# State scan of a fused kernel: B and C rows loaded apart, block steps moved, and du*B of nine states made by ScalarE and TensorE

## The reference, cut to what matters

```python
def step(h, inp):
    d_t, B_t, C_t, u_t = inp
    dA = jnp.exp(d_t[..., None] * A)
    h = dA * h + (d_t * u_t)[..., None] * B_t[:, None, :]
    y = jnp.einsum('ben,bn->be', h, C_t)
    return (h, y)
```

## Time and profile before

| | us |
|---|---|
| median of 3 runs | 665.01 (663.41 to 665.39) |
| profiled execution, whole | 662.23 |
| its span, first to last instruction | 660.4 |
| state scan in it, from the first product to the end of the last scan | 229.27 to 472.1 |

### The profile page before, as it was taken

How to read it: one execution, slowest core, us unless ns; L and a number is a source line. 1 busy time by engine, 2 the same in 40 slices (tenths; PEclk the granted TensorE clock), 3 DMA queues, 4 the chain that set the end, 5 groups by cost and what they waited for, 6 DMA issues and landing times.

```text
span 660.4 us, 9558 instructions
## 1 busy us (share of the span) xinstructions
PE 529.6 (80%) x3244; PEld 415.0 (63%) x3244; DVE 453.6 (69%) x987; ACT 334.9 (51%) x622; POOL 374.9 (57%) x306
## 2 busy tenths in 40 slices
PE   8988888997959495559546966898787889898994
PEld 5666558996837353447345735543356789898974
DVE  3444682653613799979897999999868554545585
ACT  3444551442413679644984596788150344444444
POOL 1011106455455178997898599789641666566640
PEclk9989998997988887759965995899898999999997
DMA  4234002742121455544225434534100111111213
GB/s 128 76 137 161 30 1 58 254 156 60 49 53 51 126 192 175 171 165 161 106 103 189 140 129 131 176 133 154 48 18 4 41 41 45 41 40 43 73 62 94
DMA packets 33679, 66.29 MB, mean 100 GB/s; under 512 B 6449, under 2 KB 20342, under 8 KB 33120
## 3 DMA queue, kind: packets, MB, share of 16 engines
q1 hardware_dynamic: 27136, 44.31, 20.6%
q0 software_dynamic: 4768, 9.32, 5.6%
q10 hardware_dynamic: 1728, 12.06, 5.1%
HBM read 57.60 MB, written 8.52 MB: 100 GB/s over the span
## 4 chain that ended last, share of the span: by engine, by line
PE 39%; DVE 17%; POOL 15%; issue 13%; ACT 7%; another core or an unknown queue 6%; DMA 2%; POOLq 0%; DVEq 0%; ACTq 0%
POOL w L2119 6%; PE ps L762 5%; PE ps L734 5%; PE ps L770 5%; PE ps L746 4%; PE ps L738 4%; POOL wide L2119 4%; DVE wide L1978 3%; DVE ps L1971 2%; PE ps L828 2%; DVE w L1978 2%; DVE work L1650 1%; DMA w<-bc_rows 1%; POOL work L2081 1%
## 5 line engine op out<-in xcount | busy, mean ns | idle before, releaser
L2207 POOL DMA_INDIRECT rows<-xn_rows,source x78 | 77.0, 987 | 81.2 <-DVE place L1659 24.8
L1978 DVE TENSOR_TENSOR_SCAN wide<-work,ps 128x512 f32<-128x512 f32 x86 | 99.8, 1203 | 0.4 <-ACT work L1356 0.4
L1971 DVE TENSOR_TENSOR ps<-ps,w 128x512 f32<-128x512 f32 x128 | 81.6, 684 | 6.2 <-DMA w<-bc_rows 6.0
L2119 POOL TENSOR_TENSOR wide<-wide,w 128x1024 f32<-128x1024 f32 x22 | 52.0, 2362 | 28.0 <-DVE wide L1978 27.8
L1356 ACT ACTIVATE work<-work,a_neg 128x512 f32<-128x512 f32 x86 | 56.6, 710 | 14.2 <-DVE wide L1978 6.5
L1709 DVE TENSOR_TENSOR wide<-wide,ps 128x512 f32<-128x512 f32 x39 | 26.8, 687 | 51.3 <-PE ps L738 29.1
L926 PE MATMUL ps<-ident,w 128*128 128x128 f32 x192 | 36.7, 354 | 26.4 <-POOL w L2119 26.4
L1699 DVE COPY xT<-ps 128x128 f32<-128x128 f32 x78 | 22.1, 286 | 50.8 <-remote 23.9
L762 PE MATMUL ps<-xT,wide 128*128 128x128 f32 x312 | 44.9, 290 | 10.1 <-DVE xT L1699 8.3
L926 PEld LDWEIGHTS ps<-ident,w 128*128 128x128 f32 x192 | 30.2, 185 | 35.2 <-POOL w L2119 32.3
L926 PE MATMUL ps<-ident,wide 128*128 128x128 f32 x192 | 32.5, 325 | 24.4 <-POOL wide L2119 24.3
(11 more groups left out here) (347 smaller groups left out, 1261.7 us busy)
## 6 DMA issues: line engine op xcount, KB each, us to landing
w<-bc_rows SPq DMA_DIRECT2D x64, 512.0 KB, 3.8
w<-in_w ACTq DMA_DIRECT2D x2, 2304.0 KB, 9.2
wg<-in_wg ACTq DMA_DIRECT2D x1, 2304.0 KB
wu<-in_wu ACTq DMA_DIRECT2D x1, 2304.0 KB
wd<-in_wd ACTq DMA_DIRECT2D x4, 576.0 KB
w<-y_choice SPq DMA_DIRECT2D x8, 256.0 KB, 2.8
y_slots<-yout SPq DMA_DIRECT2D x20, 64.0 KB
rows<-xn_rows,source POOLq DMA_INDIRECT x78
```

The source lines that it names most:

```text
L1971: V.tensor_tensor(dbu[:, h, :], du[:, h, :], bc_all[j % 4][:, 0:S], ALU.mult).then_inc(dbu_set, 1)
L1978: V.tensor_tensor_scan(st[n % 3][:, h, :], dA[n % 3][:, h, :], dbu[:, h, :], 0.0, ALU.mult, ALU.add).then_inc(st_set if h else st_half, 1)
L2119: G.tensor_tensor(hc[j % 4][:, 0:own, :], st[n % 3][:, 0:own, :], bc_all[j % 4][:, S:2 * S].unsqueeze(1).to_broadcast([P, own, S]), ALU.mu ...
L2207: G.indirect_dma_start(out=xin[i % RING][:, :], out_offset=None, in_=xn_rows, in_offset=bass.IndirectOffsetOnAxis(ap=source[:, i:i + 1], a ...
```

## The change

B and C rows are loaded by two DMAs of 256 KB each. B's waits for VectorE's product (`dbu_set`), C's for GpSimd's (`hc_set`), and C's of a state waits in SyncE's program for B's of the same state to have landed.

In nine states the product du*B is made otherwise (`TERM_AT`). Once per block TensorE transposes du (time onto partitions) and B, and ScalarE copies both to SBUF (`turn_du`, `turn_b`, `keep_turned`). For such a state, ScalarE multiplies the four turned tiles by a column of B as its scale (`weigh_term`), and TensorE transposes the result back into `dbu`, four tiles for each half (`turn_term`), each half after the scan of the state before that reads it. VectorE then issues no product in that state.

Steps move: `gate_sum` j = 1 to 2, `take_back` 3 to 4, `take_rows` 4 to 5, `row_stats` 5 to 6, `activate` 5 to 6, `take_low` and `project_low` 6 to 7, `soft_parts` and `project_dt` 7 to 8, `apply_norm` 10 to 11, `project_z` from 10 and 11 to 9 and 10, the first part of `step_size` 8 to 9, `scale_fetched(3)` 5 to 4; all eight `fetch` stand in block 0. The du of block 0 is made by GpSimd once more, in SBUF. Some small buffers are laid side by side for the turned tiles.

```diff
+        du_T = [w[:, NE * HID + k * EI:NE * HID + (k + 1) * EI] for w in (w1, w2) for k in range(2)]
+        term_T = [w[:, k * EI:(k + 1) * EI] for w in (y_buf, att_w) for k in range(2)]
+        b_T = xT[0][:, 0:QT * NS]
...
+        TERM_AT = ((12, 14), (5, 14), (5, 14), (5, 9, 12))
+        TURN_DU_AT = (3, 2, 2, 0)
+        KEEP_DU_AT = (4, 3, 3, 0)
+        STORE_AT = 12
+        FETCH_AT = (4, 5, 6, 7, 8, 10, 14, 15)
...
+            def spread_c(n):
+                k = n % 4
+                sp.wait_ge(bc_loaded[k], 32 * (n // 4) + 16)
+                if n >= 4:
+                    sp.wait_ge(hc_set, n - 3)
+                sp.dma_start(bc_all[k][:, S:2 * S], bc_rows[n:n + 1, S:2 * S].to_broadcast([P, S])).then_inc(bc_loaded[k], 16)
...
                     if n >= 4:
-                        sp.wait_ge(hc_set, n - 3)
-                    sp.dma_start(bc_all[j % 4], bc_rows[n:n + 1, :].to_broadcast([P, 2 * S])).then_inc(bc_loaded[j % 4], 16)
+                        sp.wait_ge(dbu_set, EH * (n - 3 - terms_up_to(n - 3)))
+                    sp.dma_start(bc_all[j % 4][:, 0:S], bc_rows[n:n + 1, 0:S].to_broadcast([P, S])).then_inc(bc_loaded[j % 4], 16)
+                    if j == STORE_AT and b < NB - 1:
+                        store_rows(b + 1)
+                    if j > 0:
+                        spread_c(n - 1)
...
+            def turn_du(b):
+                pe.wait_ge(step_set, b + 1)
...
+                for q in range(QT):
+                    for h in range(EH):
+                        last = tr(ps[:, LOOSE[q // 2], q % 2 * EI + h * P:q % 2 * EI + (h + 1) * P], u1[:, h, q * P:(q + 1) * P], ident[:, :])
+                    if q % 2:
+                        last.then_inc(du_turned.sem, 1)
+            def turn_term(n):
+                k = terms_up_to(n)
+                pe.wait_ge(*weighed.at(k + 1))
+                for h in range(EH):
+                    pe.wait_ge(st_set if h else st_half, n)
+                    for q in range(QT):
+                        last = tr(dbu[:, h, q * P:(q + 1) * P], term_T[q][:, h * P:(h + 1) * P], ident[:, :])
+                    last.then_inc(term_ps.sem, 1)
...
+                    if j == TURN_DU_AT[b]:
+                        turn_du(b)
+                        turn_b(b)
                     if j >= 2:
                         add_up(b * NS + (j - 2), j - 2)
+                    if j + 1 in TERM_AT[b]:
+                        turn_term(b * NS + j + 1)
...
+            def keep_turned(b):
+                for k in range(2):
+                    act.wait_ge(*du_turned.at(2 * b + k + 1))
+                    cp((w1, w2)[k][:, NE * HID:(NE + 1) * HID], bank(LOOSE[k])).then_inc(du_kept.sem, 1)
+                act.wait_ge(*b_turned.at(b + 1))
+                cp(b_T, ps[:, LOOSE[0], 0:QT * NS]).then_inc(b_kept.sem, 1)
+            def weigh_term(n):
+                k, j = terms_up_to(n), n % NS
...
+                for q in range(QT):
+                    last = cp(term_T[q], du_T[q], scale=b_T[:, q * NS + j:q * NS + j + 1])
+                last.then_inc(weighed.sem, 1)
...
-                    if (b, j) in ((0, 1), (1, 5)):
+                    if (b, j) in ((0, 1), (1, 4)):
                         scale_fetched(b + 2)
...
-                    if after and j == 3:
+                    if after and j == 4:
                         take_back(b - 1)
...
+                    if j == KEEP_DU_AT[b]:
+                        keep_turned(b)
+                    if j + 2 in TERM_AT[b]:
+                        weigh_term(b * NS + j + 2)
...
-                for h in range(EH):
+                for h in range(0 if turned else EH):
...
-                    dve.wait_ge(dbu_set, EH * n + h + 1)
+                    if turned:
+                        dve.wait_ge(*term_ps.at(EH * k + h + 1))
+                    else:
+                        dve.wait_ge(dbu_set, EH * (n - k) + h + 1)
...
-                        if after and j == 1:
+                        if after and j == 2:
                             gate_sum(b - 1)
...
-                    if b == 0 and 4 <= j < 8:
-                        fetch(3 * QT + (j - 4) // 2, j % 2)
-                    if b == 1 and j < 4:
-                        fetch(3 * QT + 2 + j // 2, j % 2)
-                    if j in (8, 10, 11, 12) and b < NB - 1:
+                    if b == 0 and j in FETCH_AT:
+                        fetch(3 * QT + FETCH_AT.index(j) // 2, FETCH_AT.index(j) % 2)
+                    if j in (9, 10, 11, 12) and b < NB - 1:
                         next(size)
```

More of the change, by code:

```diff
@@ L108, in build @@
         before = sb("before", [P, P])
-        wq = sb("wq", [P, D]); wk = sb("wk", [P, D]); wv = sb("wv", [P, D]); woT = sb("woT", [P, D])
-        wqk = sb("wqk", [P, D]); wvo = sb("wvo", [P, D])
+        att_w = sb("att_w", [P, 4 * D])
+        wq, wv, woT, wvo = (att_w[:, k * D:(k + 1) * D] for k in range(4))
+        wk = sb("wk", [P, D]); wqk = sb("wqk", [P, D])
         gate = [sb(f"gate{l}", [P, NE]) for l in range(2)]
@@ L173, in build @@
         DOWN_AT = 3080
-        yout = [sb(f"yout{k}", [P, D]) for k in range(4)] + [pre[:, k, :] for k in range(4)]
+        y_buf = sb("y_buf", [P, 4 * D])
+        yout = [y_buf[:, k * D:(k + 1) * D] for k in range(4)] + [pre[:, k, :] for k in range(4)]
         work = sb("work", [P, 12 * 1024])
@@ L385, in build, with terms_up_to @@
         GATE_AT = (1, 5, 8, 11)
+        TERM_AT = ((12, 14), (5, 14), (5, 14), (5, 9, 12))
+        TURN_DU_AT = (3, 2, 2, 0)
+        KEEP_DU_AT = (4, 3, 3, 0)
+        def terms_up_to(n):
+            return sum(1 for m in range(n) if m % NS in TERM_AT[m // NS])
+        STORE_AT = 12
+        FETCH_AT = (4, 5, 6, 7, 8, 10, 14, 15)
         LN_EXP = "natural_log_exp_and_others"
@@ L992, in shared_early, with turn_b @@
                         start=True, stop=True).then_inc(early_ps if w is wg else wide_ps, 1)
+            def turn_du(b):
+                pe.wait_ge(step_set, b + 1)
+                pe.wait_ge(zs_set, (b + 1) * EH)
+                if b < NB - 1:
+                    pe.wait_ge(xnT_set, b + 2)
+                if b >= 2:
+                    pe.wait_ge(*nT_set[1].at(b - 1))
+                    pe.wait_ge(*logits_set[1].at(b - 1))
+                for q in range(QT):
[3 more added lines that the diff above has]
+                        last.then_inc(du_turned.sem, 1)
+            def turn_b(b):
+                pe.wait_ge(*du_kept.at(2 * b + 1))
+                pe.wait_ge(bc_set, b + 1)
+                own = slice(DTR, DTR + NS)
+                for q in range(QT):
+                    last = tr(ps[:, LOOSE[0], q * NS:(q + 1) * NS], bc[own, q * P:(q + 1) * P], ident[own, own])
+                last.then_inc(b_turned.sem, 1)
+            def turn_term(n):
[6 more added lines that the diff above has]
+                    last.then_inc(term_ps.sem, 1)
             def states(b):
@@ L1017, in states @@
                         convolve(b + 1, j - 4)
-                    if before and j == 6:
+                    if before and j == 7:
                         project_low(b + 1)
-                    if before and j == 7:
+                    if before and j == 8:
                         project_dt(b + 1)
-                    if before and j in (10, 11):
-                        project_z(b + 1, j - 10)
+                    if before and j in (9, 10):
+                        project_z(b + 1, j - 9)
                     if after and j == 13:
@@ L1301, in soft_parts, with soft_rest @@
                     last.then_inc(relu_set, 1)
[L1302 to L1303 removed]
+            def soft_rest(x):
+                act.wait_ge(act_step, steps.n)
+                steps.link(A(u2, u1, ACT.Exp, scale=-1.0))
+                steps.link(A(u1, u2, ACT.Identity, bias=1.0))
+                A(u3, u1, ACT.Copy, bias=-1.0).then_inc(soft_one, 1)
             def soft_exp():
@@ L1398, in states @@
                         scale_rows(b + 1)
-                    if before and j == 1:
+                    if before and j == 2:
                         take_xnT(b + 1)
@@ L1964, in state @@
             def state(n, j, between):
-                dve.wait_ge(bc_loaded[j % 4], 16 * (n // 4 + 1))
+                turned, k = j in TERM_AT[n // NS], terms_up_to(n)
+                if not turned:
+                    dve.wait_ge(bc_loaded[j % 4], 32 * (n // 4) + 16)
                 if n >= NS and j == 0:
                     dve.wait_ge(du_set, n // NS)
-                for h in range(EH):
+                for h in range(0 if turned else EH):
                     if n >= 1:
@@ L1987, in between @@
                             added_stats(b + 2)
-                        if after and j == 1:
+                        if after and j == 2:
                             gate_sum(b - 1)
-                        if after and j == 5:
+                        if after and j == 6:
                             row_stats(b - 1)
```

51 lines of the change are left out of this document (32 added, 19 removed).

## The result

The changed kernel took 687.62 us, median of 6 runs (681.9 to 691.0), against 664.47 us for the kernel before, 6 runs of the same session (663.4 to 667.0). The ratio is 1.0329, 95% interval 1.0291 to 1.0368. I had forecast 677 with a range to 685: the sign was right, the loss nearly twice as large as my sum, and the time lies above the range.

A forecast was written before the change was run, and what follows sets the result against it. VectorE bounds the scan stage, GpSimd the ends of blocks 0 and 1. Late turned products leave a lag of 12.3 us at scan 63, added to the median 665.0: forecast 677 us, range 663 to 685.

The forecast's parts named there:

- What bounds: After gate_sum, VectorE idles ahead of scans 21, 37 and 53 by 10.3, 7.9 and 6.1 us, released by turned tiles.
- Block 0: GpSimd's gathers cost 3.1 us more; gate_sum(0) begins at 298.2, scan 18 at 299.3, net 0.3 us gained.
- swallowed by GpSimd: Block 0: the turned products of 12 and 14 and earlier loads of B gain nothing, since GpSimd is full.
- Block 1, the step that failed: Chain from gate_sum to the turned product of state 5: take_back at 11.7 us, then TensorE 7.1, 19.4 in all.
- that rule: TensorE idle for take_back may fall to half rate: the 7.1 us stay by the row, up to 14 by the rule.
- Blocks 2 and 3, the same term: Chains from gate_sum to the turned state 5: 17.0 us in block 2, 15.2 in block 3.
- The ends of blocks: Lag shrinks toward block ends: 7.2 to 4.9 us in block 1, 11.7 to 9.7 in 2, 14.7 to 12.3 in 3.
- the 0.8 of the decay: Block 2, state 41: a 0.8 us wait for a decay goes, lag 11.7 to 10.9.
- the 1.2 that I let the later gate_sum give back: Block 2's end: one state's step of gate_sum to j = 2 returns 1.2 us, leaving a lag of 9.7 at scan 50.
- States 12, 14, 30, 46, 57, 60: 12, 14, 30 and 46 gain nothing through GpSimd or waits for sums; 57 and 60 gain 2 x 1.18 us.
- The half clock after new waits: Rival, chance 0.14: TensorE at half clock costs about 5 us each in blocks 1 and 2, making 687.
- The faster case: Rival, chance 0.14: every turned product in time, 652.8 us; needs TensorE's chain after gate_sum under 9.1 us.

The follow-up runs named there:

- back_first: Changed kernel with ScalarE's take_back ahead of the weighing in blocks 1 to 3, nothing else; ratio 1.0131 to the kernel before.
- no_fives: Changed kernel with VectorE's products again in states 5 of blocks 1 to 3, the six other states still turned; 665.58 us, ratio 1.0024 to the kernel before.
- no_terms: Changed kernel without any turned product, du and B still turned and kept; 664.18 us, ratio 1.0012 to the kernel before.
- no_turning: Changed kernel without turned products and without turning or keeping du and B; ratios 0.9929 and, measured again, 0.9903 to the kernel before.

## Where the prediction was right, and the step that failed

**What bounds.** Right: the loss is VectorE's idle time after gate_sum, released by turned tiles. The idle ahead of the three states 5 was 13.15, 10.00 and 7.18 us, forecast 10.3, 7.9 and 6.1. The rest is a matter of size: at scan 63 the lag was 24.7 us, forecast 12.3, and the median rose by 23.2 us. Chains below are counted from the start of the first scan after gate_sum.

**Block 0.** Nearly right: gate_sum(0) ended at 302.95, 300.2 with the 2.7 taken off, and scan 18 came 0.5 us late where I had 0.3 early. State 14 waits 6.22 us; I had named it as swallowed by GpSimd, and so it is, or the scan would be far more than 0.5 late. The clock there was 0.50, before 0.56.

**Block 1, the step that failed.** Down to take_back I was right to 0.1 us: it ends at 314.55, 11.7 us after scan 18 began, as forecast, and the weighing takes 1.62 us for my 1.6. The next item was "project_out, half the convolution and one `add_up` 7.1 (302.27 to 309.33)". It took 9.74 us (314.69 to 324.43). The 7.1 were read where TensorE worked without a pause at a granted clock of 1.00; here it had stood 3.96 us. project_out alone took 5.25 us against 2.75, at a granted clock of 0.50, which is the lower of the two levels, 1.2 GHz. So the chain was 22.3 us, not 19.4. In back_first, where only the place of take_back differs and the pause is gone, the same instructions take 2.75.

The Trainium skill, TensorE: Matmul & The Clock Gate (Part 1: The HAM clock gate), says that an array left idle is put back to half rate. I had weighed that rule and left the sum at the row's 7.1 us. The trace agrees with it for the pause of 3.96 us. Behind the one of 1.90 us in block 2 project_out ran at full rate; behind 2.28 us in block 3 it began at full rate and went over to half rate on the way, and took 4.13 us (the first row to the last):

```profile
455.58 0.46 PE L916 MATMUL ps<-x_all,wqk 128*128 128x128 f32 x2 [2.28 <-ACT w L1142]
...
459.71 2.15 PE L951 MATMUL ps<-w,ident 128*128 128x512 f32 x4
```

**Blocks 2 and 3, the same term.** In block 2 it was add_skip that began at half clock (0.63 us for a pair of 128x128 products, later 0.39). It took 4.86 us, where block 1's took 3.26, and that is most of why the chain up to take_back took 11.2 us against 9.3:

```profile
378.22 2.07 PE L1002 MATMUL ps<-work 128*128 128x512 f32 x2 [1.27 <-DVE work L2003]
...
383.08 1.04 PE L1035 MATMUL ps<-ident,work 128*128 128x128 f32 x8
```

In block 3 take_back ended 11.0 after gate_sum for my 10.2, a decay kept VectorE 1.5 us on the way, and what follows took 6.85 for 5.0, of which project_out's half clock is 1.4. Chains: 19.2 for 17.0 and 18.0 for 15.2. The three overruns are 2.9 + 2.2 + 2.8 = 7.9 us, and TensorE at half clock is 2.5 + 1.6 + 1.4 = 5.5 of them. The sum had priced every TensorE item of the three chains at full clock.

**The ends of blocks.** The second term in error. I let the lag shrink by 2.3, 2.0 and 2.4 us from the scan after the chain to the block's end. It shrank by 1.1 (10.9 to 9.8), 1.2 (18.8 to 17.6) and 0.7 (25.4 to 24.7), 3.7 us less in sum. In block 1 GpSimd was late itself: its product of state 25 began at 344.94, 10.5 us later than before with the 2.7 taken off, where I had 6.4. From there to the end of its last product of the block, 374.07, it took 29.1 us, as forecast (29.0); the turned state 30 then came 3.0 us behind the product of 27 and not 2.5. In block 2 the 0.8 of the decay did come back, but of the 1.2 that I let the later gate_sum give back only some 0.2: scan 50 stands behind gate_sum in both kernels. In block 3 the 2.4 were the products of 57 and 60; 57 gained; 60, after a wait of 1.60 us, came 3.92 us behind the scan before it, 0.5 more than in a full stream with products. That is the 1.7 that is missing.

With the 0.8 us of block 0 the sum closes: 12.3 + 7.9 + 3.7 + 0.8 = 24.7 us at scan 63, which is what the trace has (497.20 - 469.81 - 2.7).

**States 12, 14, 30, 46, 57, 60.** Right as a sum: no_fives against no_terms gives 0.1% for all six, in a kernel without the states 5. For 57 and 60 see above.

**What I left out.** The turning and keeping of du costs 4 us of stage where no product is turned (no_terms against no_turning); I had it only as items inside the chains. In the changed kernel it is partly in the rows of the chains and can't be added to the sum above. On the other side, steps and rows gave 3.0 back, which the sum had only as waits that go.

**Rivals.** The half clock after new waits stood at 687 with a chance of 0.14, and by its number it is the nearest. Its mechanism is shown, with a smaller price than I gave it: behind the new waits 2.5 us in block 1's project_out and 1.4 in block 3's, none in block 2's, where I had 10 in all. That its 687 met the measured 687.6 is luck: most of the missing time came from the other terms above. The faster case fell on the condition it named: the chain took 18.0 to 22.3 us where 9.1 were allowed, and even in back_first 15.3 to 15.5 from the end of gate_sum.

## What to carry to other kernels

Before giving work of the bounding engine to two others, walk the two in program order from the last event that releases them to the moment the result is wanted, and compare that with what the bounding engine has to do meanwhile; here 1.18 us of products saved in a state stood against a chain of 18 to 22 us where 9.1 were free. A duration of TensorE read where it ran without a break need not hold behind a new pause: price it at both clocks. When a wait is removed at one state, look at what is wanted one state later on the same chain: with the turned product ahead, 7.5 us of waiting turned up at row_stats and 14.9 at decays.

## What the runs showed of the hardware that I had not expected

- The length of TensorE's pause for take_back doesn't by itself say at which clock project_out runs. The 14 traces hold three project_outs each. The 34 behind no pause, or one of up to 1.90 us, all took 2.67 to 2.76 us. Of the 8 behind 2.15 to 3.98 us, six took 4.13 to 5.25 us; the two behind 2.15 us (no_terms, eights) took 2.76 and 2.75, but that behind 2.16 in no_fives took 4.38. These two rows are of block 1 in no_terms and in no_fives, where the same first pair of products takes 0.46 and 0.69 us. What else decides stays open.

```profile
311.48 0.46 PE L916 MATMUL ps<-x_all,wqk 128*128 128x128 f32 x2 [2.15 <-ACT w L1142]
```

```profile
307.94 0.69 PE L916 MATMUL ps<-x_all,wqk 128*128 128x128 f32 x2 [2.16 <-ACT w L1142]
```

- ScalarE's copy of 128x256 with a factor per partition takes 0.40 us (two in 0.81, from 308.31 to 309.13), about midway between 0.31 for 128x128 and 0.54 for 128x512.
- Two chips differed outside the stage and hardly in it: no_turning took 659.5 and 621.0 us on them, with scan stages of 240.4 and 239.3 us.
